# Dots of a DLRM tower in two parts, and one embedding feature of three tiles read row by row by the sync engine

## What is computed

```python
e = jnp.stack([tbl_f[ids[:, f]] for f in range(27)], axis=1)   # 2048 x 27 x 128
dot = jnp.einsum('bnd,bmd->bnm', e, e)                          # 27 x 27 dot products a sample
z = dot[:, pairs j > i]                                         # 351 of them
h = jnp.concatenate([z, dense_ctx], axis=1)                     # 367 columns
h = jnp.maximum(h @ W_top1 + b_top1, 0.0)                       # 512
h = jnp.maximum(h @ W_top2 + b_top2, 0.0)                       # 256
y = h @ W_top3                                                  # 1
```

## Time and profile before

| | us |
|---|---|
| median of 3 runs | 588.62 (588.22 to 590.11) |
| the profiled execution | 590.46 |
| its span in the profile | 588.6 |
| PE busy | 399.7 (68% of the span) |
| weight loads busy | 360.4 (61%) |
| DVE busy | 248.6 (42%) |
| GpSimd busy | 270.0 (46%) |
| ACT busy | 163.6 (28%) |

### The profile page before, as it was taken

The page is one execution under the profiler, slowest core; times in us unless marked ns, Lnnn a source line. Parts: engine busy times, 40 slices in busy tenths (PEclk is TensorE's granted clock), DMA queues, the critical chain, the costliest instruction groups (busy, mean ns, idle before and its releaser), DMA issues.

```text
span 588.6 us, 13981 instructions
## 1 busy us (share of the span) xinstructions
PE 399.7 (68%) x6083; PEld 360.4 (61%) x6083; DVE 248.6 (42%) x770; ACT 163.6 (28%) x217; POOL 270.0 (46%) x286
## 2 busy tenths in 40 slices
PE   4520176657595876949687685948778487969776
PEld 3420156557484775838586574938667476959665
DVE  5500224636244462506544262625635163647112
ACT  3210223314233222412324031422223132334241
POOL 6777462627446252645526164453536264530000
PEclk9855586958588686968879597887878697989898
DMA  8932130445213121321213022221213122210000
GB/s 196 246 87 59 35 79 20 111 126 139 55 46 72 29 72 29 71 52 50 68 30 82 22 64 57 51 73 29 73 38 77 34 55 69 54 34 2 2 2 2
DMA packets 23004, 36.65 MB, mean 62 GB/s; under 512 B 6224, under 2 KB 17120, under 8 KB 22944
## 3 DMA queue, kind: packets, MB, share of 16 engines
q0 software_dynamic: 8896, 18.24, 12.8%
q1 hardware_dynamic: 14048, 17.52, 11.8%
HBM read 35.73 MB, written 0.01 MB: 61 GB/s over the span
## 4 chain that ended last, share of the span: by engine, by line
PE 61%; issue 19%; another core or an unknown queue 9%; ACT 5%; DVE 2%; DMA 2%; SPq 1%; ACTq 0%; DVEq 0%
PE embT_ps L371 29%; PE gram_ps L397 12%; PE h_ps L426 7%; PE h_ps L450 5%; PE embT_ps L381 4%; ACT embT L575 2%; PE flat_ps L409 2%; PE embT_ps L366 2%; DMA embT<-in_tbl 2%; ACT embT L567 2%; DVE one_hot L493 2%; ACT tbl L555 1%; SPq L290 1%; SPq L282 0%
## 5 line engine op out<-in xcount | busy, mean ns | idle before, releaser
L340 POOL DMA_INDIRECT emb<-in_tbl,idx x272 | 263.5, 969 | 249.5 <-PE embT_ps L381 153.8
L371 PE MATMUL embT_ps<-one_hot,tbl 125*128 125x256 f32 x1284 | 214.1, 328 | 52.7 <-DVE one_hot L493 28.2
L493 DVE TENSOR_SCALAR one_hot<-ids,row_of 125x256 fp32r<-125x256 int32 x658 | 197.3, 371 | 108.9 <-PE embT_ps L371 47.9
L371 PEld LDWEIGHTS embT_ps<-one_hot,tbl 125*128 125x128 f32 x1284 | 195.5, 228 | 62.7 <-issue 30.7
L397 PE MATMUL gram_ps<-embT 128*27 128x27 f32 x4096 | 72.8, 217 | 97.5 <-issue 90.0
L397 PEld LDWEIGHTS gram_ps<-embT 128*27 128x27 f32 x4096 | 58.5, 129 | 113.4 <-issue 104.1
L567 ACT COPY embT<-embT_ps 128x256 f32<-128x256 f32 x77 | 52.1, 677 | 227.6 <-PE embT_ps L371 161.7
L575 ACT COPY embT<-embT_ps 128x512 f32<-128x512 f32 (+1 forms) x80 | 87.0, 1091 | 19.9 <-PE embT_ps L381 10.9
L521 DVE STREAM_TRANSPOSE flat<-gram_ps 128x864 f32<-128x864 f32 x16 | 17.3, 1083 | 169.2 <-PE gram_ps L397 169.2
L381 PE MATMUL embT_ps<-ident,emb 128*128 128x128 f32 x272 | 46.5, 288 | 29.8 <-ACT embT L567 22.4
L381 PEld LDWEIGHTS embT_ps<-ident,emb 128*128 128x128 f32 x272 | 34.3, 149 | 31.5 <-issue 31.0
(11 more groups left out here) (38 smaller groups left out, 75.1 us busy)
## 6 DMA issues: line engine op xcount, KB each, us to landing
ids<-in_ids_hot SPq DMA_DIRECT2D x77, 128.0 KB
emb<-in_tbl,idx POOLq DMA_INDIRECT x272
embT<-in_tbl SPq DMA_DIRECT2D x5, 448.0 KB
w_sb<-in_tbl SPq DMA_DIRECT2D x3, 560.0 KB
w_sb<-in_W_ring SPq DMA_DIRECT2D x1, 756.0 KB
w_sb<-in_W_top SPq DMA_DIRECT2D x1, 512.0 KB
h1T<-in_tbl SPq DMA_DIRECT2D x1, 448.0 KB
w_sb<-in_tbl SPq DMA_DIRECT2D x1, 448.0 KB
```

The source lines that it names most:

```text
L340: pool.indirect_dma_start(gathered_row(t, s), None, tables[f][:, :], bass.IndirectOffsetOnAxis(ap=idx[:, t, f:f + 1], axis=0),).then_inc(g ...
L371: mm = pe.matmul(out[:, 0:HN], tbl[0:ROWS, part, AT[o] + chunk, :], one_hot[0:ROWS, k % SLOTS, c, :], start=(chunk == 0 and part == 0), st ...
L493: done = dve.tensor_scalar(one_hot[0:ROWS, k % SLOTS, c, :], of, row_of[0:ROWS, KINDS.index(CH[o]), chunk:chunk + 1], None, ALU.is_equal)
```

## The change

The dots of a tile are issued in two parts of 16 groups (128 of the 256 matmul instructions, one PSUM bank) each: the first where the whole stood, behind quad 0, the second behind quad 2, ahead of the second layer step. In the last tile the second part of dots 14 stands behind quad 0 and ahead of `layer1`; in END `layer2` of tile 14 stands between the two parts of dots 15. DVE's transposes still come after the second part.

In tiles 5, 10 and 15 the feature of slot 16 (the only one of quad 4) is not gathered by GpSimd. SyncE reads its 128 ids of the tile in four stretches of 32: it loads 32 ids from HBM into registers and issues 32 loads of one row (512 bytes) each, addressed by the registers, to a buffer of its own, `one_by_one`. The stretches stand in SyncE's order behind id loads 20, 25, 30 and 35 for tile 5, 45, 50, 55 and 60 for tile 10, and 62, 67, 72 and the end of the loads for tile 15 (`due`). PE waits for all 128 rows before quad 4 of these tiles. GpSimd skips both that gather and the wait ahead of it.

```diff
+BY_ROW = (5, 10, 15)
+STRETCH = 32
...
+def by_row_feature(feats):
+
+    return feature_order(feats)[feats - max(READ_IN_HALF) - 1]
...
+    def gathers(t, q):
+
+        return [s for s in quad(t, q) if not (t in BY_ROW and s == GF - 1)]
+
     def rows_landed(t, q):
 
-        return sum(len(quad(s, q)) for s in range(t % EB, t + 1, EB))
+        return sum(len(gathers(s, q)) for s in range(t % EB, t + 1, EB))
...
         if t > 0:
-            dots = [[("dots", t - 1, 0, GROUPS32)]]
+            dots = [[("dots", t - 1, 0, GROUPS32 // 2)], [], [("dots", t - 1, GROUPS32 // 2, GROUPS32)]]
...
-            return [("flat", t - 2), *dots[0], ("layer1", t - 3), ("quad", t, 0), ("layer1", t - 2),
+            return [("flat", t - 2), *dots[0], ("layer1", t - 3), ("quad", t, 0), *dots[2], ("layer1", t - 2),
...
-    END = [("dots", T - 1, 0, GROUPS32), ("layer2", T - 2), ("ring", T - 1), ("flat", T - 1), ("layer1", T - 1),
+    END = [("dots", T - 1, 0, GROUPS32 // 2), ("layer2", T - 2), ("dots", T - 1, GROUPS32 // 2, GROUPS32), ("ring", T - 1), ("flat", T - 1), ("layer1", T - 1),
            ("layer2", T - 1)]
...
+    STRETCHES = TILE // STRETCH
+
+    def due(n):
+        done = []
+        for i, t in enumerate(BY_ROW):
+            last = min(len(HOT0) + O * (t + 1) // HT - 2, len(HOTS))
+            done += [i * STRETCHES + m for m in range(STRETCHES) if last - O // HT * (STRETCHES - 1 - m) == n]
+        return done
...
+        one_by_one = sb("one_by_one", [P, 2, D])
...
         def gathered_row(t, s):
+            if t in BY_ROW and s == GF - 1:
+                return one_by_one[:, BY_ROW.index(t) % 2, :]
...
+            row_ids = [sp.alloc_register(f"row_id{i}") for i in range(STRETCH)]
+            f_row = by_row_feature(FEATS)
+
+            def read_rows(m):
+
+                n, r = divmod(m * STRETCH, TILE)
+                t = BY_ROW[n]
+                if n > 1 and r == 0:
+
+                    sp.wait_ge(turned, TURNED["quad", BY_ROW[n - 2], QUADS - 1])
+                sp.load(row_ids, ids_hot[O:O + 1, t * TILE + r:t * TILE + r + STRETCH])
+                for i in range(STRETCH):
+                    row = sp.snap(row_ids[i], min_val=0, max_val=tables[f_row].shape[0] - 1)
+                    sp.dma_start(one_by_one[r + i:r + i + 1, n % 2, :],
+                                 tables[f_row][bass.ds(row, 1), :]).then_inc(row_landed[n % 2], 16)
...
+                for m in due(n):
+                    read_rows(m)
+            for m in due(len(HOTS)):
+                read_rows(m)
...
-                    if t >= EB:
+                    if t >= EB and gathers(t, q):
                         pool.wait_ge(turned, TURNED["quad", t - EB, q])
-                    for s in quad(t, q):
+                    for s in gathers(t, q):
...
             def turn(t, q):
-                pe.wait_ge(gathered[t % EB][q], 16 * rows_landed(t, q))
+                if gathers(t, q):
+                    pe.wait_ge(gathered[t % EB][q], 16 * rows_landed(t, q))
+                if len(gathers(t, q)) < len(quad(t, q)):
+                    pe.wait_ge(row_landed[BY_ROW.index(t) % 2], 16 * TILE * (BY_ROW.index(t) // 2 + 1))
...
-    arrays["ids_hot"] = np.ascontiguousarray(ids.T[list(ONE_HOT)])
+    arrays["ids_hot"] = np.ascontiguousarray(ids.T[[*ONE_HOT, by_row_feature(feats)]])
```

More of the change, by code:

```diff
@@ L249, in dlrm_tower @@
         gathered = [[sem(f"gathered{b}_{q}") for q in range(QUADS)] for b in range(EB)]
+        row_landed = [sem(f"row_landed{b}") for b in range(2)]
         turned = sem("turned")
```

## The result

Measured on the chip: 646.5 us median (645.02 to 647.64, 4 runs) against 589.37 us (588.22 to 596.67, 4 runs), ratio 1.094 with a 95% interval of 1.085 to 1.103. Forecast were 650 us, with a range of 603 to 695, and "slower". The profiled execution took 645.02 us for a span of 643.2, 54.6 us more than before.

What follows compares the result with a forecast made beforehand. PE's own instruction stream was taken to bound the kernel, the dots being its worst stretch. Terms -45 + 96 + 13 - 5 - 2.5 + 5.5 = +62 us, added to the 588.62 us median, gave 650 us, range 603 to 695.

Steps and rivals of the forecast that it cites:

- (b): Second part behind quad 2, beside released gathers: slow phase makes it cost 7.4 us in each of 13 tiles, 96 us more.
- (a): First part behind quad 0: half the products and the fetch hole go, over 13 tiles 45 us less.
- (c): Granted clock: a second low stretch per tile, behind the second part, 1.0 us net each, 13 us more in all.
- (d): Three last dots stretches, without gathers beside them: short parts save holes and a little clock, together 5 us less.
- (e): GpSimd issues three gathers fewer, shortening the slow phase by a slot in two of three: 2.5 us less.
- (f): SyncE's 384 one-row loads and register reads: PE waits for rows in tiles 5 and 10, 5.5 us more.
- Second part undisturbed: Rival: second part behind quad 2 has no slow phase, costs 1.7 us and no clock; 578 us, chance 0.20.
- SyncE's row loads slow PE like gathers: Rival: SyncE's row issues hold PE in second parts, 12 us instead of 7.4; about 700 us, chance 0.09.
- Row loads are slow to issue: Rival: at 1.2 us a row, tiles 5 and 10 wait some 30 us each; 705 us, chance 0.06.
- the halved case: Rival: slow phase in the second part half as long, costs and gains nearly cancel; 603 us, chance 0.07.
- the likeliest case: Whole kernel, terms as summed: 650 us, with its own bounds giving 625 to 685; chance 0.58.

Runs made afterwards that it cites:

- E6: Kernel before, GpSimd running memsets instead of the gathers of tiles 2 to 15 (zeros in place of rows): 454.2 us.
- e7: Kernel before, gathers of tiles 2 to 15 replaced by plain loads of 128 fixed rows, issued by GpSimd behind the same waits: 455.6 us.
- e9: Kernel before, SyncE loading the 17 features of tiles 2 to 15 as plain fixed blocks, GpSimd gathering only tiles 0 and 1: 461.2 us.
- E3: Kernel before plus one wait: GpSimd holds gathers of quads 3 and 4 and those queued behind until the dots are complete: 607.6 us against 584.3.
- e4: Kernel before with dots split, no row loads, GpSimd holding quad 1's gathers and those behind until the second part is complete: 627.5 us, ratio 1.067.
- e1: Kernel before with only the dots split in two parts, no row loads, GpSimd gathering all features: 626.2 us, ratio 1.074.
- e8: Kernel before with dots whole, plus the change's row loads, each stretch five id loads (one tile) earlier: ratio 1.016.
- e5: Kernel before with dots split only in the last two tiles and END, where GpSimd has almost no gathers left: 579.9 us, ratio 0.994.

## Why the prediction was right, and where it was not

The total was 0.5% off, the direction and the mechanism of (b) held, and yet single terms were off in both directions.

- **The slow phase comes from gathers (step b's ground): right, and too narrow.** E6, e7 and e9 show it and narrow it to what a gather has and a plain load of adjoining rows has not. I had priced it as something that happens to dots. E3 and e4 show that it happens to other steps beside a run of gathers too, and to ACT and DVE, and that moving the gathers moves the cost.
- **(b), price of the second part: undersized.** 118.8/13 = 9.1 us against 7.4, just over the upper bound of 9. In the part at 328.37 the slow phase outlasted the last gather by 1.7 us, not 0.95.
- **(a), gain of the first part: undersized.** The first parts took 79.5 us where 140.6 - 45 = 96 were forecast. Four of the 13 took 1.1 to 1.7 us beside held-up gathers, which I had not foreseen. That the fetch hole goes is right: outside the slow phases the longest hole in any part is 0.6 us. The 23 us for it were a little high; the trace before has eleven holes of 1.5 to 2.1 us and one of 0.4 in these tiles, 20.4 us. And the four short parts were not all gain: the layer steps behind them have the 16.7 us of holes, a cost that the sum did not have.
- **(c), clock: the mechanism right, the net too high.** From 85 to 571 us the granted clock falls to 0.50 26 times, twice a tile as forecast; from 84 to 500 us of the kernel before it fell 20 times. L475 is busy for 57.9 us instead of 43.2, but L417 for 197.8 instead of 214.1. In all PE's busy time without the dots is 0.2 us less, against 13 us more forecast. The price of 1.8 us a layer also rests on a step that ran only in part at the lower clock: behind the 4.41 us at 552.20 it was granted in full again from 555.4.
- **(a) to (d) together** were forecast at 59 us; the split alone cost 7.4% of 588.6, 43 us. What made it cheaper is a term that the sum put at nothing: PE's idle time before hot reads and quads, when it waits for DVE and ACT. It was 52.7 + 29.8 us and is 38.2 + 20.9 in e1, 23 us less (in the changed kernel 33.1 + 25.2, without the waits for rows). With PE held longer in the dots, DVE and ACT get further ahead; that this is the reason is argued, not tested.
- **(d): right.** From the start of the dots of tile 13 to the end 66.9 us became 60.8, 6 us less against 5. In END itself nothing is won: from the start of the last dots to the end it is 18.1 us instead of 17.1, since the chain of DVE's transposes and ACT's ring copy is no longer covered by `layer2`.
- **(e) and (f): undersized.** Forecast +3 us, measured 1.094 against 1.074, about 12 us; (e) was not tested by itself. The register read, from the end of the id load to the first row load, took 5.0 us in the late stretch of tile 5 and 5.0 to 7.1 us in all twelve, against 5. But a row took 18.27/32 = 0.57 us in that stretch, and 0.52 in the mean of all (13.6 to 22.4 us a stretch), not 0.38:

```profile
249.87 18.27 SPq L331 DMA_DIRECT2D one_by_one<-in_tbl  x32
...
333.16 17.99 SPq L331 DMA_DIRECT2D one_by_one<-in_tbl  x32
```

  PE waited 10.7 us instead of 5.5 (the two terms, 3.8 and 1.9, make 5.7). And I had counted the loads beside the waits at nothing but 0.2 MB; e8 prices them at 9 us.
- **The rivals.** "Second part undisturbed" fell: the shortest of the 13 second parts took 7.9 us. "SyncE's row loads slow PE like gathers" fell as put: in e8 32 row loads went out from 315.44 to 335.76, beside the whole dots of 321.9, which took 13.9 us as against 13.8 for the same tile before, and e8's dots in all were no longer. A milder form of it is the 1.6% of e8. "Row loads are slow to issue" fell as well (0.52 us a row in the mean, not 1.2), and so did the halved case: no second part was shorter than 7.9 us.
- **The range.** 625 to 685 for the likeliest case is narrower than its bounds give: (b), (c) and (f) all at their ends make 613 to 705.

So the 0.5% is luck in part: 16 us too much for the split against 9 too little for the rows.

## What to carry to other kernels

Before moving a stretch of many short matmuls, look at what GpSimd issues in its new place, and price indirect gathers by what they cost the whole kernel (here 0.54 us each), not by GpSimd's idle time; holding them back, in the two ways tried here, didn't save it. Where no gathers run, break up a long stretch of short matmuls, here 256 instructions into twice 128 with other steps between: that was worth 61 of 461 us, of which the holes alone were 43.4 us. A split that is good in one part of a kernel can be bad in another; e5 keeps it where it is good.

## What the runs showed of the hardware

- Indirect gathers of 128 rows issued by GpSimd delayed PE's instructions and ACT's and DVE's starts (ACT by 8.4 us at 554.34 in the changed kernel): 588.6 us of span against 453.8 with plain loads of the same size from the same queue. GpSimd took 2.12 us for four plain loads in several stretches, 0.53 us each; a gather takes 0.94 us and 0.30 behind it.
- In the trace of the kernel before each of the 14 long holes in dots (1.5 to 2.4 us) ends 2.1 to 2.7 us after a packet on the queue for instructions has started, which bears out the reading as a wait for the program. The hole was 2.0 to 2.8 us in 14 of e9's 16 stretches, 4.10 and 5.33 us in the other two. During the longest (108.3 to 111.1 us) the queues moved 109 GB/s, during one of 2.70 us (210.7 to 213.5) 10 GB/s; that traffic is the cause isn't shown, since one with 29 GB/s took 2.09 us.
- Single gathers took 4.4 to 7.1 us in the changed kernel, one every 74 to 82 us, and 6.7 to 7.07 in e1, one every 75 to 77; nine first parts of dots beside them took 1.1 to 1.7 us. Five plain loads of e7 took 5.3 to 5.4 us, so it is not only gathers.
- Reading 32 registers from HBM took SyncE 5.0 to 7.1 us, 5.7 in the mean of twelve. The Trainium skill (Runtime: NRT & Kernel Launch, Instruction fetch mechanics) has about 200 ns a register. The trace agrees: 157 to 222 ns.
